# Adding the causal mask of a diagonal block with one 128-row product in place of two 64-row products

## What is computed

```python
qkv = x @ w_qkv
q, k, v = jnp.split(qkv, 3, axis=-1)
q = q * cos + _rotate_half(q) * sin
k = k * cos + _rotate_half(k) * sin
att = jnp.einsum('bhtd,bhsd->bhts', q, k) * scale
att = jnp.where(causal, att, jnp.finfo(att.dtype).min)
att = jax.nn.softmax(att, axis=-1)
y = jnp.einsum('bhts,bhsd->bhtd', att, v)
return y.transpose(0, 2, 1, 3).reshape(B, T, C) @ w_proj
```

## Time and profile before

| what | value |
|---|---|
| median of 3 runs | 659.97 us (659.73 to 662.86) |
| time of the profiled execution | 657.28 us |
| its span, first to last instruction | 655.5 us |
| causal stage with masks (steps 0 to 7, first score to last sum) | 280 to 547 us |
| PE, PEld, DVE, ACT, POOL busy | 596.2, 417.8, 475.7, 348.1, 160.8 us |
| products of line 1661 | 512, 47.6 us busy |
| mean granted TensorE clock | 0.956 |

### The profile page before, as it was taken

One profiled execution on the slowest core, in us unless ns is written; L12 is line 12 of the kernel. 1 busy time (PEld: TensorE's weight loads), 2 busy tenths in 40 slices (PEclk: granted clock), 3 DMA queues, 4 the chain that ended last, 5 costly groups with the idle time before them and its releaser, 6 DMA issues. The chain is left out here.

```text
span 655.5 us, 12421 instructions
## 1 busy us (share of the span) xinstructions
PE 596.2 (91%) x4320; PEld 417.8 (64%) x4320; DVE 475.7 (73%) x1493; ACT 348.1 (53%) x713; POOL 160.8 (25%) x332
## 2 busy tenths in 40 slices
PE   1996879999998969999999999999999997999997
PEld 0885767888878856654545353645453545888887
DVE  5577866588697767879787779788879432876764
ACT  3855456323334643577676667676767674222221
POOL 7631534020033437613233121211120100000000
PEclk9999899999999995579999799999999999999999
DMA  8000000233322200000000000000000002333332
GB/s 296 4 0 1 1 0 1 70 98 130 114 80 85 80 1 2 0 1 1 2 1 1 1 2 1 2 0 2 1 1 1 1 1 67 99 124 121 114 123 73
DMA packets 18669, 27.98 MB, mean 43 GB/s; under 512 B 2984, under 2 KB 7208, under 8 KB 18608
## 3 DMA queue, kind: packets, MB, share of 16 engines
q1 hardware_dynamic: 17888, 25.85, 12.1%
q10 hardware_dynamic: 720, 1.34, 0.6%
HBM read 25.85 MB, written 1.33 MB: 41 GB/s over the span
## 5 line engine op out<-in xcount | busy, mean ns | idle before, releaser
L831 ACT ACTIVATE arena<-bank 128x512 f32<-128x512 f32 (+3 forms) x384 | 166.2, 496 | 68.9 <-PE bank L1661 45.9
L1691 PE MATMUL bank<-kza,qta 64*128 64x512 f32 (+3 forms) x384 | 138.0, 447 | 5.6 <-DVE work L1201 3.5
L1198 DVE CUSTOM_DVE_ANT_0 bank<-bank,mask_qk 128x512 f32<-128x512 f32 (+3 forms) x256 | 119.4, 518 | 32.4 <-PE bank L1691 32.0
L1649 PE MATMUL bank<-qtb,kza 64*128 64x512 f32 (+3 forms) x384 | 134.6, 411 | 4.3 <-ACT arena L831 1.8
L1691 PEld LDWEIGHTS bank<-kza,qta 64*128 64x128 f32 x384 | 65.2, 202 | 79.5 <-DVE work L1198 42.4
L761 ACT ACTIVATE work<-bank 128x512 f32<-128x512 f32 x80 | 47.7, 598 | 112.8 <-PE bank L1321 111.6
L1201 DVE TENSOR_REDUCE work<-bank 128x1 f32<-128x512 f32 x128 | 80.3, 683 | 18.6 <-PE bank L1691 18.6
L1537 PE MATMUL bank<-dw,work 128*128 128x128 f32 x640 | 85.7, 278 | 2.5 <-DVE work L1128 2.5
L1124 DVE TENSOR_TENSOR work<-work,bank 128x512 f32<-128x512 f32 x80 | 54.7, 684 | 45.6 <-PE bank L1321 40.8
L1537 PEld LDWEIGHTS bank<-dw,work 128*128 128x128 f32 x640 | 81.8, 193 | 6.8 <-issue 2.9
L1649 PEld LDWEIGHTS bank<-qtb,kza 64*128 64x128 f32 x384 | 65.2, 188 | 29.0 <-ACT arena L831 17.0
(11 more groups left out here) (195 smaller groups left out, 1056.9 us busy)
## 6 DMA issues: line engine op xcount, KB each, us to landing
kt<-cw_rows SPq DMA_DIRECT2D x160, 128.0 KB, 2.9
x<-x_in SPq DMA_DIRECT2D x4, 256.0 KB, 7.3
y_out<-x SPq DMA_DIRECT2D x4, 256.0 KB, 3.1
arena<-gw_in SPq DMA_DIRECT2D x1, 640.0 KB, 9.8
arena<-uw_in SPq DMA_DIRECT2D x1, 640.0 KB, 8.7
dw<-dw_in SPq DMA_DIRECT2D x1, 640.0 KB, 9.5
work<-q_in SPq DMA_DIRECT2D x2, 256.0 KB, 7.7
arena<-const_in ACTq DMA_DIRECT2D x1, 400.0 KB, 6.7
```

The costliest lines, as they stand in the source:

```text
L831: act.activation(pb[:, blk % 2, h, 0:w], s_bank(n)[:, 0:w], ACT.Exp, scale=SCALE).then_inc(p_ready, 1)
L1198: ins = dve.tensor_tensor_reduce(out=src, in0=src, in1=mask_qk[:, CW - w:], scale=1.0, scalar=-3e38, op0=ALU.add, op1=ALU.max, accum_out=dst)
L1649: ins = pe.matmul(s_bank(n)[:, 0:w], kz(s, h, j // CT)[pair(h), j % CT * P:(j % CT + 1) * P], qtb[pair(h), s % 2, (c + 1) * CW - w:(c + 1) ...
L1691: pe.matmul(a_bank(n)[:, 0:w], qta[pair(h), slot(b, g), i * P:(i + 1) * P], kz(s, h, half)[pair(h), 0:w], start=True, stop=True).then_inc( ...
```

## The change

One product now adds the mask of a head: weights `mask_qk[:, CW - P:]` (128 rows, 128 columns, the same bf16 mask that the maxima use) and all 128 columns of the 128-row identity. `BLOCK_ORDER` is the same. `mask_kq`, its cast and its 256 columns of `const_in` are gone.

```diff
-C_ID, C_MA, C_MB, C_BM, C_HS, C_IO, C_COS, C_SIN, C_END = 0, 128, 256, 512, 640, 656, 672, 736, 800
+C_ID, C_MA, C_BM, C_HS, C_IO, C_COS, C_SIN, C_END = 0, 128, 256, 384, 400, 416, 480, 544
...
-        mask_kq = sb("mask_kq", [P, 2, P], BF16)
...
-            pool.tensor_copy(mask_kq[:, :, :], raw_c[:, C_MB:C_MB + 2 * P].rearrange("p (a n) -> p a n", a=2))
...
                     c, j = B_BLOCKS[k]
-                    r = pair(S_HEADS[order])
                     n = (s * NBLK + k) * GH + order
                     if j >= 4 * c:
-                        for a in range(2):
-                            ins = pe.matmul(s_bank(n)[:, a * 2 * SL:(a + 1) * 2 * SL], mask_kq[r, a, :], identb[r, r],
-                                            start=False, stop=True, skip_group_check=True)
-                        ins.then_inc(b_full, 1)
+                        pe.matmul(s_bank(n)[:, 0:P], mask_qk[:, CW - P:], identb[:, :], start=False, stop=True,
+                                  skip_group_check=True).then_inc(b_full, 1)
...
-    for a in range(2):
-        c[:, C_MB + a * P:C_MB + (a + 1) * P] = np.where(r[None, :] > (r[:, None] % (2 * SL) + a * 2 * SL), -1e30, 0.0)
```

## The result

The kernel after takes 670.83 us in the median of four runs (668.09 to 675.63) against 659.85 us before (659.56 to 662.86). The ratio is 1.020, with a 95% interval of 1.015 to 1.025: slower by 11.0 us, where 12.9 was forecast. A second set of four runs on another occasion gave 1.022 (1.018 to 1.026). The profiled execution took 668.96 us, its span is 667.1.

A forecast was written before the change was run, and what follows sets the result against it. TensorE was taken as busiest, with VectorE waiting for its masked maxima products. Of 31.5 us added raw, 12.9 was put on the path; with the 659.97 median that made 672.9 us, 8 in 10 for 664 to 692.

The forecast's parts named there:

- The bound: Causal stage, step 5: VectorE waits for maxima products at seven places in blocks 1, 2, 3, 9, 10 and 11.
- The array empties: Each change between 64-row and 128-row products: 0.09 us, taken from a bracket of 0.07 to 0.14.
- The pair: Masks 0 and 1 of a masked block: cost goes from 0.15 to 0.41 us, 0.26 added.
- The load of a 128-row bf16 weight: Ahead of each mask product: 0.01 us exposed, the unknown; its other end was the fp32 load's exposed 0.10.
- Mask 2: Ahead of the sums in a masked block: cost goes from 0.08 to 0.16 us, 0.08 added.
- Mask 3: Last mask of a block: 0.20 us added, about 0.01 where 128-row work follows, in blocks 1 and 3.
- What lies on the path: Causal steps: 1.55 us in each of seven, 2.0 in the last, 12.9 us in all.
- The rest: The cast, smaller constants' DMA (400 to 272 KB) and 256 fewer loads and products: no effect on the time.
- the raw 31.5 us: Rival: all added TensorE time in the 64 masked blocks shows, 691.5 us; chance 0.14.
- VectorE doesn't cover it all: Judges the rival that VectorE's work hides the added time in the causal stage, 660 to 662 us; chance 0.12.
- bound by issue: Rival: a mask costs its starts, not columns; 256 fewer products save 7.7 us, 652 us; chance 0.05.
- The clock's rival: Causal stage: TensorE could lose its clock again, one more stretch costing up to 3.3 us, 676 us; chance 0.07.

The follow-up runs named there:

- the two experiments: Kernel after with two 128-row products of 64 columns per head: 674.34 us; kernel before with one 64-row product of 128 columns, half the mask's rows left out: 655.72 us.
- the repeat: The kernel before, run once more unchanged: 659.38 us, ratio 1.004 to before.
- the late order with 128 rows: Kernel after with masks 0 and 1 moved behind the third pair of scores, next to mask 2: 665.84 us, ratio 1.015 to before.

## Why the prediction was right, step by step

- **The bound.** TensorE and VectorE take turns in the causal stage, and the added time shows where VectorE waits for maxima. It held in sum, 3.96 us instead of 2.95. Six of the seven places grew, and the first of block 2 shrank from 0.66 to 0.59. The new one in block 0 is the only one that I had ruled out.
- **The array empties between 64-row and 128-row products, 0.09 us.** Measured as 0.09 from the end of the second pair to the masks, and 0.16 from mask 2 to the sums (0.06 to 0.07 of columns and 0.09). The square of the two experiments shows that the rows make the difference. In block 8 the gap stands ahead of the mask's load, and the halves end within 0.01 us of each other, so neither the wide load nor the wait for the other half makes it. That the array empties in it is inferred; no row shows it.
- **The pair, 0.26 added a block.** The third score's columns start 0.42 behind instead of 0.15: 0.27. Right where the third score doesn't wait for ScalarE; in blocks 3, 10 and 11 it does, and nothing is added to the distance.
- **The load of a 128-row bf16 weight, 0.01.** Line 1657's loads are 95 to 96 ns long, as the 64-row ones before. The unknown took the value of its nearest row, and the end of 0.10 was not reached.
- **Mask 2, 0.08 added.** This term was mis-sized: from the third score to the sums it measures 0.09 to 0.16 a block, 1.02 us a step, of which 0.82 shows when it stands alone. My walk had far more of it under cover.
- **Mask 3, 0.20, and 0.01 where 128-row work follows.** This one was too small as well: it measures 0.25 to 0.26 in five of the six blocks, and 0.01 in block 0. Alone it adds 0.36 us a step; blocks 1 and 3 don't grow, as I had it.
- **What lies on the path, 1.55 us a step and 2.0 in the last, 12.9 in all.** Measured 1.47 in steps 5 and 6, 1.21 to 1.64 in 1 to 4, 2.36 in step 0 and 1.74 in the last, 12.8 in all. The sum is right to 0.1, partly by luck: I had 0.8 at block 4 and it is 0.60 (the blocks grew by 0.35, -0.28, 0.61, -0.08), and 0.75 for blocks 8 to 11, where it is 0.87; mask 2 and mask 3 were too small, and the pair's share on the path too large.
- **The time, 672.9 us.** That 670.83 came so near is partly luck too. The median of four lies halfway between two runs with a granted clock of 0.957 and 0.959 (668.96 and 668.09 us) and two with 0.949 and 0.944 (672.69 and 675.63), and the sum has no term for the clock.
- **The rest.** `const_in` is 272 KB and lands in 6.5 us instead of 6.7; nothing came of it. The stretch before step 0 is 2.8 us longer and the one after step 7 is 1.0 shorter than in the first profile of before; neither is the change's. In kernels with 64-row masks or none step 0 starts at 279.8 to 285.0 us, and the time after step 7 is 107.4 to 107.6 us in profiles without a stretch at half clock there and 108.3 to 108.5 in those with one of 3.4 us.
- **The rivals.** Not all of the raw 31.5 us shows, since the pair's share is mostly covered. VectorE doesn't cover it all. The products aren't bound by issue: 256 fewer are worth 0.1 us a step. The rule of about 62 ns for each product that the Trainium skill gives (page "TensorE: Matmul & The Clock Gate", section "Back-to-back issue gap") was no guide here: by it, as an estimate, 32 products fewer would save 2.0 us a step, and they save 0.1. The clock's rival, with a chance of 0.07, did come in on top of the forecast, in step 0: about 5 us in a part of the runs. I had read the clock as 1.00 in the rest of the stage, from one window; it was 0.90 in step 0 too, whose first 7 us belong to the stretch at half clock, and that is the stretch that grew.

## What to carry to other kernels

Count a product by the rows of the array that it takes away from its neighbours, not by its instructions: between 64-row products in both halves, one 128-row product costs a gap of 0.09 us on either side and an exposed fp32 load, 0.23 to 0.27 us here, and halving the number of small bf16 products gains 3 to 4 ns apiece. What of it shows depends on where it stands: ahead of a place at which TensorE waits anyway, most vanishes; straight ahead of the work that the other engine waits for, most of it shows. Take places out one at a time before trusting a sum of terms, for in the plain step the dearest one showed an eighth of its price and the cheapest one four fifths. Then look at the other steps too: over the eight steps the pair cost 5.3 us.

## What was not expected of the hardware

With the changed masks in step 0 the stretch at 1.2 GHz at the head of the causal stage lasted 54.6 to 58 us in three of four profiles, instead of 41 us or less, and that cost 5 us there, more than the masks cost in any later step. In the later steps, which have the same masks and begin at 2.4 GHz, the granted clock stayed at 1.00 in both profiles of after.

That isn't so in all profiles, and with masks of either kind. TensorE fell to 1.2 GHz once within the later steps in five of the fourteen: for 6.8 us in step 2 of before (34.51 us instead of the repeat's 31.44), in step 7 with mask 2 alone and in step 6 of the late order with 128 rows, and for 3.4 us in step 7 with one 64-row product and in step 7 with 128 rows from step 1 on. Nothing here shows that 128-row masks make such falls more frequent.

The Trainium skill, page "TensorEngine Tiling (Array Packing)", section "Key Properties", says that changing the tiling mode drains TensorE. The trace agrees in that no product starts for 0.09 us on each side of the 128-row masks, beyond what their columns take; that this is the draining it doesn't show.
